# First x load in the set-up, flag sum, next layer norm and keep load inside the first stage's tail, weights loaded by the second stage

## The chip, the cores and the metric

One core of one Trainium2 chip runs the whole program. The metric is the device time of one execution in microseconds (us); about 14 us (0.5%) is what a measurement of this kernel can tell from no change. The engines are TensorE (PE, with its weight loads PEld), VectorE (DVE), ScalarE (ACT), GpSimd (POOL) and SyncE (SP, which issues every data transfer here).

## What is computed

Sixteen graphs (G = 16) of N = 1024 nodes with 128 features. Two layers, each with a residual:

```
h = max(layernorm(x), 0)
for W, b in three:                      # layer 0
    h = h @ W + b;  nh = h / max(|h|, 1e-12)
    h = (adj * (nh @ nh.T)) @ h         # relu after the first two
x = x + h                               # x1 below
h = max(layernorm(x), 0)                # layer 1
keep = dilate(adj > 0, mask)            # row by row, 1024 sequential steps
adj_d = adj * keep
h1, h2, h3 = three times: bn(relu(sage(., adj_d)))   # agg / degree, two projections, row norm
x = x + (concat(h1, h2, h3) @ Wl + bl) * mask
```

`keep` depends on `adj` alone. `bn` needs statistics over all graphs, so layer 1 is cut into stages.

## The kernel before, in words

The program is a row of blocks. In each block every engine runs its own list in order, and the block ends when all engines have come to its end: a barrier. The blocks are: `setup` (constants, the mask), `layer0`, `changed`, `dilate_all` under a condition, `weights`, `layer1_first`, `layer1_second`, `layer1_third`, `final`.

**layer0** does layer 0 of all graphs and, between its steps, the dilation. A graph is three units (`UNITS`, 48 in all, two graphs side by side). One step of a unit is `cos` (a 128x512 piece of nh nh^T: three matmuls on PE into one of two PSUM banks), then the product with adj on DVE into one of four `ew` buffers, then `agg` (PE). A `cos` on PE waits for the product two steps back, an `agg` for its own product. The kernel is written out from a plan: `Planner.order` takes steps with a cost, a rank and what they come after, and gives each engine its list. The names in it are: `lna` and `lnb` (layer norm on DVE: statistics, then subtract and scale), `lnc` (transpose of it), `posta` and `postb` (transpose of the result on PE, add to x on DVE; then SP stores x1), `fill` and `row` (the loads of adj for the dilation; a `fill` is then turned into 8 bits by POOL, a `row` by ACT), `base`, `rank`, `rule`, `drop`, `wide` (the dilation of a block of rows), `check` (writes a flag if a block's rounds did not settle), and `mask` (four transposes on PE, one DVE operation, and a store of 64 KB of keep from one of three `kp` buffers). Each SP list is strict: a load that waits holds back all behind it. The block ends on SP with waits for the last x1 store and the last keep stores.

**changed** is a block of its own: DVE sums the flags, PE adds them over the partitions with a matmul, DVE writes the integer `flag`. Then all engines load `flag` into a register and jump over `dilate_all` if it is 0, as it is here.

**weights** is a block with three loads by SP (W 768 KB, rows 640 KB as a broadcast, cols), on which its end waits; DVE fills `onesf` and `mf2`.

**layer1_first** takes the graphs in `ORDER` (14, 15, 0, 1, ...; the adj of graphs 14 and 15 is still in SBUF). For n = 0, `load(0)` brings x1 and keep of graph 14; DVE's `prep(0)` does its layer norm and then eight products adj * keep (`mk`, L1388); PE's first aggregation needs ReLU of the layer norm (`ln(0)` on ACT) and these products one by one; POOL adds the eight products for the degree (`dsum`), which PE sums at L1304; the projections with `W` come behind that.

Of the kernel before, what the change touches and what calls it, by code (L numbers as in the profile page):

```python
# [11 lines left out]
U8 = mybir.dt.uint8  # L12
# [90 lines left out]
def build(nc, A):  # L103
    with ExitStack() as top:
# [14 lines left out]
        C["flag"] = sb("flag", [128, 1], I32)  # L119
# [6 lines left out]

        C["adj"] = [sb(f"adj{i}", [128, NK, N]) for i in range(2)]
        setup(nc, A, C)
        layer0(nc, A, C, S)
        unsettled = changed(nc, C)  # L130
# [11 lines left out]
        weights(nc, A, C)  # L142
# [9 lines left out]
def setup(nc, A, C):  # L152
    with ExitStack() as ctx:
# [22 lines left out]
        def dve(e):  # L176
            e.memset(C["eps"][:], 1e-5)
            e.memset(C["flags"][:], 0.0)
# [20 lines left out]


def weights(nc, A, C):
    with ExitStack() as ctx:
        P = Scope(nc, ctx, "w")
        S = P.sems("loads")

        def sp(e):
            e.dma_start(C["W"][:], A["W"]).then_inc(S["loads"], 16)
            e.dma_start(C["rows"][:], A["rows"].partition_broadcast(128)).then_inc(S["loads"], 16)
            e.dma_start(C["cols"][:], A["cols"]).then_inc(S["loads"], 16)
            e.wait_ge(S["loads"], 48)  # L210

        def dve(e):
            e.memset(C["onesf"][:], 1.0)
            e.tensor_tensor(C["mf2"][:], C["mf"][:], C["mf"][:], ALU.mult)

        run(nc, dve=dve, sp=sp)
# [97 lines left out]
def plan_units(P):  # L314
# [10 lines left out]
    def prepare(v):  # L325
# [4 lines left out]
        if i == 0:  # L330
            if g > 1:
                transfer(("lnload", g), 1400, [("pe", "hf", v - 1)], rank=1)
            x = ("dma", "xfirst", 1) if g == 1 else ("dma", "lnload", g)
            add("dve", ("lna", g), 2070, 1, soon + [x])
# [26 lines left out]
    def agg(idx):  # L361
# [20 lines left out]
    post(3 * G - 2, [("pe", "agg", 16 * (3 * G - 1) + 1)])  # L382
    post(3 * G - 1, [])
# [69 lines left out]
def layer0_plan():  # L453
    P = Planner()
    plan_units(P)
    plan_dilation(P)
    return P.order({"D0": 1, "D1": 1, "ats0": 1, "ats1": 1, "af": 3, "v": 3, "kp": 3})


def layer0(nc, A, C, S):  # L460
    with ExitStack() as ctx:
# [3 lines left out]
        T = P.sems("ats0 ats1 at af0 af1 af2 sign low au x bs b0 ct ru vr sd v8 wb wd av rw tr kp kps0 kps1 kps2")  # L465
# [7 lines left out]
        tmp = P.sb("tmp", [128, NK, 128])  # L473
# [9 lines left out]
        ats = [P.sb(f"ats{i}", [128, 4, 128]) for i in range(2)]  # L483
        af = [P.sb(f"af{i}", [128, 512]) for i in range(3)]
# [47 lines left out]
        def sp(e):  # L532
# [3 lines left out]
            for kind, *a in plan["sp"]:  # L536
# [5 lines left out]
                elif kind == "lnload":  # L542
                    g, = a
                    if g:
                        e.wait_ge(E["tnh"], 6 * (g // 2) + g % 2)
# [3 lines left out]
                elif kind == "xload":  # L549
                    g, = a  # L550
                    if g == 0:
                        e.wait_ge(E["lnr"], 2)
                    else:
                        e.wait_ge(E["xs"], 16 * g)
                    e.dma_start(flat2(xt), A["x"][g]).then_inc(E["xld"], 16)
# [4 lines left out]
                elif kind == "fill":  # L560
# [4 lines left out]
                    e.dma_start(ats[h][:], A["adjT"][quad * Q + i][half(h), blk(k)].rearrange(  # L565
                        "(q p) n -> p q n", p=128)).then_inc(T[f"ats{h}"], 16)
                elif kind == "row":
# [4 lines left out]
                    e.dma_start(af[r % 3][:], A["adj"][n // NK * Q + i, blk(n % NK), half(j)]).then_inc(  # L572
                        T[f"af{r % 3}"], 16)
                elif kind == "mask":
# [4 lines left out]
                        T[f"kps{c % 3}"], 16)  # L579
            e.wait_ge(E["xs"], 16 * G)  # L580
# [3 lines left out]
        def pool(e):  # L584
            for kind, *a in plan["pool"]:
# [4 lines left out]
                e.tensor_scalar(TT[:, Q * (quad % 2) + i, 4 * h:4 * h + 4, blk(k)].bitcast(U8), ats[h][:], 0.0, ONE8,  # L590
                                ALU.is_gt, ALU.mult).then_inc(T["at"], 1)

        def pe(e):
# [11 lines left out]
            def take(bank, step):  # L605
                if users[bank]:
# [5 lines left out]
                    elif kind == "wide":  # L612
                        e.wait_ge(T["av"], nth["act", "wide", a[0], a[1], a[2]])
                    else:
                        e.wait_ge(T["kp"], nth["dve", "mask", a[0], a[1], a[2], a[3]])
# [1273 lines left out]
```

## Time and profile before

| what | value |
|---|---|
| median of 3 runs | 2811.43 us (2810.03 to 2820.57) |
| the profiled execution: its own time / its span | 2813.71 / 2811.9 us |
| PE / DVE / ACT / POOL busy | 2666.9 / 2183.0 / 1273.8 / 1092.8 us |
| mean granted TensorE clock | 0.981 |

The span runs from the first to the last instruction on the core; the execution's own time is 1.8 us longer. The profiled execution is 2.3 us above the median. Times in rows count from the start of the span.

### The profile page before, as it was taken

The numbers are of one execution on the slowest core, as the hardware profiler recorded it, in microseconds if no ns is written. First come the engines' busy times: TensorE is split into PE (matmuls) and PEld (weight loads), VectorE is DVE, ScalarE is ACT, GpSimd is POOL, SyncE is SP. The second block draws the span as 40 slices with busy tenths as digits, with TensorE's granted clock in tenths as the row PEclk, the third lists the DMA queues.
The fourth block names the chain that finished last, engine by engine and source line by source line (L and its number), as shares of the span: only waits on it lengthen the run. The fifth ranks groups of instructions, "written<-read, shape, count | busy, mean of one in ns | idle before, by whom it ended". The sixth has DMA issues, their size and how long they took to land. (4 is left out here: it accounts for less than half of the span.)

```text
span 2811.9 us, 41242 instructions
## 1 busy us (share of the span) xinstructions
PE 2666.9 (95%) x13446; PEld 1692.4 (60%) x13446; DVE 2183.0 (78%) x5582; ACT 1273.8 (45%) x3780; POOL 1092.8 (39%) x493
## 2 busy tenths in 40 slices
PE   6999999999999999999999968999999879999997
PEld 4666666666655656666666635555555545555886
DVE  5889999999888988999998857666666336774667
ACT  2555645665454454656544302333333324443664
POOL 3635344400143465730000008666666303442661
PEclk9999999999999999999999988999999989999998
DMA  6465374462273384562251133555555129996652
GB/s 231 150 213 188 105 218 148 126 218 70 84 255 105 114 287 134 167 220 82 63 187 53 34 99 116 200 200 201 201 201 202 65 96 397 394 396 239 223 201 121
DMA packets 322510, 492.31 MB, mean 175 GB/s; under 512 B 20592, under 2 KB 214512, under 8 KB 322288
## 3 DMA queue, kind: packets, MB, share of 16 engines
q1 hardware_dynamic: 322288, 489.57, 50.5%
q8 instruction: 112, 1.84, 0.3%
q14 instruction: 110, 0.90, 0.1%
HBM read 422.38 MB, written 67.11 MB: 174 GB/s over the span
## 5 line engine op out<-in xcount | busy, mean ns | idle before, releaser
L590 POOL TENSOR_SCALAR a_T<-a_ats 128x512 uint8<-128x512 f32 x256 | 514.8, 2019 | 711.7 <-DMA a_ats<-in_adjT 710.6
L668 PE MATMUL a_acc<-a_ew,a_Hr 128*128 128x512 f32 x1536 | 758.5, 602 | 0.0
L838 DVE TENSOR_TENSOR a_ew<-adj,a_cos 128x512 f32<-128x512 f32 x768 | 505.9, 679 | 37.8 <-PE a_cos L661 36.5
L659 PE MATMUL a_cos<-a_nh 128*128 128x512 f32 x768 | 407.4, 530 | 3.1 <-DVE a_nl L830 2.8
L1434 POOL TENSOR_TENSOR b_dsum<-adj 128x1024 f32<-128x1024 f32 x16 | 142.2, 8888 | 605.8 <-DVE adj L1388 605.8
L668 PEld LDWEIGHTS a_acc<-a_ew,a_Hr 128*128 128x128 f32 x1536 | 268.5, 190 | 140.5 <-issue 104.2
L767 ACT ACTIVATE a_vr<-a_D,a_small 128x128 f16<-128x128 f32 x560 | 210.1, 456 | 248.2 <-DVE a_small L902 247.9
L777 ACT ACTIVATE a_v<-a_D,a_wb,a_small 128x256 f16<-128x256 f32 x512 | 260.2, 561 | 119.0 <-PE a_D L702 108.1
L661 PE MATMUL a_cos<-a_nh,a_nl 128*128 128x512 f32 x768 | 304.1, 396 | 0.0
L660 PE MATMUL a_cos<-a_nl,a_nh 128*128 128x512 f32 x768 | 301.6, 393 | 0.0
L1278 PE MATMUL b_acc<-adj,b_h 128*128 128x512 f32 x512 | 224.3, 596 | 21.7 <-DVE adj L1388 21.7
L1438 POOL TENSOR_TENSOR b_dsum<-b_dsum,adj 128x1024 f32<-128x1024 f32 x96 | 225.7, 2351 | 14.4 <-POOL b_dsum L1438 0.9
L1278 PE MATMUL b_acc<-adj,b_z 128*128 128x512 f32 x512 | 224.1, 596 | 0.0
L1535 PE MATMUL c_acc<-adj,c_z 128*128 128x512 f32 x512 | 222.4, 592 | 0.0
L760 ACT ACTIVATE a_Ab<-a_af 128x512 fp8e4<-128x512 f32 x256 | 156.9, 632 | 92.2 <-DMA a_af<-in_adj 90.5
L1625 POOL TENSOR_TENSOR adj<-adj,c_kp 128x1024 f32<-128x1024 f32 x52 | 102.8, 2009 | 242.3 <-DMA adj<-in_adjT 242.3
L941 DVE SCALAR_TENSOR_TENSOR a_T<-a_v,a_Ab 128x512 fp8e4<-128x512 f16 x256 | 176.9, 706 | 24.3 <-ACT a_v L777 24.0
L659 PEld LDWEIGHTS a_cos<-a_nh 128*128 128x128 f32 x768 | 145.6, 190 | 66.0 <-issue 36.3
L951 DVE SCALAR_TENSOR_TENSOR a_kp<-a_D,a_T 128x512 fp8e4<-128x512 f32 x256 | 174.3, 684 | 11.7 <-PE a_D L715 8.9
L1278 PEld LDWEIGHTS b_acc<-adj,b_h 128*128 128x128 f32 x512 | 96.5, 191 | 138.0 <-issue 112.7
L660 PEld LDWEIGHTS a_cos<-a_nl,a_nh 128*128 128x128 f32 x768 | 146.5, 191 | 54.5 <-issue 43.8
L1278 PEld LDWEIGHTS b_acc<-adj,b_z 128*128 128x128 f32 x512 | 96.7, 191 | 115.9 <-issue 115.7
(205 smaller groups left out, 4467.5 us busy)
## 6 DMA issues: line engine op xcount, KB each, us to landing
adj<-in_adjT SPq DMA_DIRECT2D x108, 1024.0 KB, 12.6
adj<-in_adjT SPq DMA_DIRECT2D x128, 512.0 KB, 4.6
a_ats<-in_adjT SPq DMA_DIRECT2D x256, 256.0 KB, 3.3
a_af<-in_adj SPq DMA_DIRECT2D x256, 256.0 KB, 3.8
scr_keep<-a_kp SPq DMA_DIRECT2D x256, 64.0 KB, 1.5
b_kp<-scr_keep SPq DMA_DIRECT2D x16, 1024.0 KB, 7.3
c_zi<-scr_z SPq DMA_DIRECT2D x32, 512.0 KB, 6.0
c_ai<-scr_ag SPq DMA_DIRECT2D x32, 512.0 KB, 6.8
```

The costliest lines, as they stand in the source:

```text
L590: e.tensor_scalar(TT[:, Q * (quad % 2) + i, 4 * h:4 * h + 4, blk(k)].bitcast(U8), ats[h][:], 0.0, ONE8, ALU.is_gt, ALU.mult).then_inc(T["a ...
L659: e.matmul(cos[j][:], n[:, blk(k)], n[:, half(j)], start=True, stop=False)
L660: e.matmul(cos[j][:], n[:, blk(k)], m[:, half(j)], start=False, stop=False)
L661: e.matmul(cos[j][:], m[:, blk(k)], n[:, half(j)], start=False, stop=True).then_inc(E["cos"], 1)
L668: e.matmul(acc[j][:], Hr[u % 2][:, k, :], ew[idx % EW][:], start=(k == 0), stop=(k == NK - 1)).then_inc(E["agg"], 1)
L767: e.activation(vr[p][:, i, :], D0[:, i, :], ACT.Abs, bias=sm[p]["b2"][:, i:i + 1], scale=sm[p]["sc"][:, i:i + 1]).then_inc(T["vr"], 1)
L777: t = e.activation(v[c % 3][:, g * 256:g * 256 + 256], D1[:, 2 * g:2 * g + 2, :].rearrange("p b c -> p (b c)"), ACT.Abs, bias=wb[p][:, i, ...
L838: e.tensor_tensor(ew[idx % EW][:], adj[g % 2][:, k, half(j)], cos[j][:], ALU.mult).then_inc(E["ew"], 1)
L941: e.scalar_tensor_tensor(TT[:, slot, 4 * j:4 * j + 4, blk(k)], v[c % 3][:].rearrange("p (q c) -> p q c", c=128), 1.0, Ab[:, slot, half(j)] ...
L1278: t = e.matmul(acc[j][:], src[:, q, :], adj[n % 3][:, q, half(j)], start=(q == 0), stop=(q == NK - 1))
L1438: e.tensor_tensor(d[:], d[:], b[:, q, :], ALU.add).then_inc(E["ds"], 1)
L1535: t = e.matmul(acc[j][:], z[m % 2][:, q, :], adj[slot(m)][:, q, half(j)], start=(q == 0), stop=(q == NK - 1))
```

## The change

1. `setup`: SP's first transfer is now x of graph 0, ahead of the mask's. `lnload 0` leaves the plan; `lna 0` waits for `xload` instead. The buffer `tmp` is now `C["h0"]`, which lives through the program.
2. `changed` is gone. Its three steps are `tally` steps in layer0's plan, on the PSUM bank `D1` (a 1x1 matmul).
3. The layer norm of graph 14 for layer 1 is done in layer0, after `postb` of its own unit 46, from `xt` in SBUF: `lna 16`, `lnb 16` on DVE, square root and ReLU (`first`) on ACT. It is written to `C["h0"]`. The load of graph 15's x into `xt` (`xload 15`) now waits for `lnb 16`.
4. The keep load of graph 14 (1 MB) is issued by SP at the end of layer0, into `kp0`, which shares its space with the staging buffers of `fill` and `row`; it waits for the last keep store of graph 14. The end of the block doesn't wait for it.
5. `weights` is gone. Its loads are issued in layer1_first behind `load(1)`; PE and DVE wait for them (`wl`) at their first use. `prep(0)` is the eight products alone.
6. In the later stages some buffers have been laid on `C["h0"]`, `kp0` and `stage`.

```diff
@@ build
+        C["h0"] = sb("h0", [128, NK, 128])
+        C["stage"] = sb("stage", [128, 5, 512])
+        C["kp0"] = C["stage"][:, 0:4, :].rearrange("p a b -> p (a b)").bitcast(FP8).rearrange("p (k n) -> p k n", k=NK)
...
-        unsettled = changed(nc, C)
+        unsettled = nc.values_load(C["flag"][0:1, 0:1], min_val=0, max_val=128 * 128 * 128)
...
-        weights(nc, A, C)
@@ setup, sp
+            e.dma_start(flat2(C["h0"]), A["x"][0]).then_inc(C["xload"], 16)
             e.dma_start(mi[:], A["mask"]).then_inc(S["mask"], 16)
@@ plan_units
-            transfer(("xload", g), 1400, [("dma", "postb", UNITS.index((g - 1, 2)))] if g else [("dve", "lnb", 1)])
-
-    transfer(("lnload", 0), 1400, (), "sp")
+            read = [("dve", "lnb", G)] if g == G - 1 else []
+            transfer(("xload", g), 1400, read + ([("dma", "postb", UNITS.index((g - 1, 2)))] if g else [("dve", "lnb", 1)]))
...
     post(3 * G - 2, [("pe", "agg", 16 * (3 * G - 1) + 1)])
+    add("dve", ("lna", G), 2070, 1, [("dve", "postb", 3 * G - 2)])
+    add("act", ("lna", G), 210, 0, [("dve", "lna", G)])
+    add("dve", ("lnb", G), 2280, 1, [("act", "lna", G), ("pe", "hf", 3 * G - 1)])
+    add("act", ("first", 0), 920, 3, [("dve", "lnb", G)])
     post(3 * G - 1, [])
@@ layer0_plan
+    add("dve", ("tally", 0), 200, 3, [("dve", "check", n) for n in range(QUADS * NK)])
+    add("pe", ("tally", 1), 200, 2, [("dve", "tally", 0)], None, "D1")
+    add("dve", ("tally", 1), 200, 3, [("pe", "tally", 1)], None, None, "D1")
+    quad, i = divmod(ORDER[0], Q)
+    P.transfer(("keep", 0), 2800, [("dma", "mask", quad, i, q, j) for q in range(NK) for j in range(2)] +
+               [("act", "row", n, i, j) for n in range(NK * QUADS) for i in range(Q) for j in range(2)])
@@ layer0, sp
+                elif kind == "keep":
...
+                    for c in range(3):
+                        e.wait_ge(T[f"kps{c}"], max(16 * (m // 3 + 1) for m in stored if m % 3 == c))
+                    e.dma_start(C["kp0"].bitcast(U8), S["keep"][ORDER[0]].rearrange("k p n -> p k n")).then_inc(
+                        C["kpload"], 16)
@@ layer1_first, sp
-            load(0)
             load(1)
+            e.dma_start(C["W"][:], A["W"]).then_inc(E["wl"], 16)
+            e.dma_start(C["rows"][:], A["rows"].partition_broadcast(128)).then_inc(E["wl"], 16)
+            e.dma_start(C["cols"][:], A["cols"]).then_inc(E["wl"], 16)
             clear(e, C["bank"][0])
             load(2)
@@ layer1_first, dve
+            def prep(n):
+                b, c = adj[n % 3], kp[n % 2]
+                if n:
+                    norm(n)
+                if n:
+                    e.wait_ge(E[f"kp{n % 2}"], 16 * (n // 2 + n % 2))
+                else:
+                    e.wait_ge(C["kpload"], 16)
```

The two plans give the same lists except for swaps of neighbours among the first hundred steps and for the tail. DVE's list at the end of layer0, from `postb 46` on (the add to `a_x`), first of the kernel before; `a_ew` is the product of a step, `a_kp` a piece of keep:

```order
L843 TENSOR_TENSOR a_x<-a_pp,a_x 128x1024
L838 TENSOR_TENSOR a_ew<-adj,a_cos 128x512
L951 SCALAR_TENSOR_TENSOR a_kp<-a_D,a_T 128x512
L838 TENSOR_TENSOR a_ew<-adj,a_cos 128x512
L951 SCALAR_TENSOR_TENSOR a_kp<-a_D,a_T 128x512
L838 TENSOR_TENSOR a_ew<-adj,a_cos 128x512 x2
L951 SCALAR_TENSOR_TENSOR a_kp<-a_D,a_T 128x512 x2
```

The same place in the changed kernel (`h` is `C["h0"]`):

```order
L866 TENSOR_TENSOR a_x<-a_pp,a_x 128x1024
L861 TENSOR_TENSOR a_ew<-adj,a_cos 128x512
L816 BN_STATS a_lnst<-a_x 128x6 x8
L819 BN_AGGR a_lnmv<-a_lnst 128x2 x8
L861 TENSOR_TENSOR a_ew<-adj,a_cos 128x512 x2
L824 RECIPROCAL a_lnrs<-a_lnsd 128x8
L829 TENSOR_SCALAR h<-a_x,a_lnmv,a_lnrs 128x128 x8
L861 TENSOR_TENSOR a_ew<-adj,a_cos 128x512
L980 SCALAR_TENSOR_TENSOR a_kp<-a_D,a_T 128x512
L861 TENSOR_TENSOR a_ew<-adj,a_cos 128x512 x2
L980 SCALAR_TENSOR_TENSOR a_kp<-a_D,a_T 128x512 x2
```

The statistics stand between the products of steps 756 and 757, the subtraction between those of 758 and 759, and the mask pieces come later: the last of them is now behind the product of the last step, just ahead of the last `postb`.

SP's list at the end of layer0, before:

```order
L559 DMA scr_x<-a_x 128x1024
L578 DMA scr_keep<-a_kp 128x512 x2
L555 DMA a_x<-in_x 128x1024
L578 DMA scr_keep<-a_kp 128x512 x7
L559 DMA scr_x<-a_x 128x1024
L85 UNCONDITIONAL_BRANCH
```

and in the changed kernel (L588 is the keep load into `kp0`):

```order
L560 DMA scr_x<-a_x 128x1024
L556 DMA a_x<-in_x 128x1024
L579 DMA scr_keep<-a_kp 128x512 x10
L588 DMA stage<-scr_keep 128x8x1024
L560 DMA scr_x<-a_x 128x1024
L85 UNCONDITIONAL_BRANCH
```

The keep load stands directly ahead of the last x1 store, on whose landing the block's end waits, and the x load stands ahead of ten keep stores instead of seven.

## Rows read from the trace of the kernel before

**Rows 1.** Page, part 1: busy us (share of the span) xinstructions.
```profile
PE 2666.9 (95%) x13446; PEld 1692.4 (60%) x13446; DVE 2183.0 (78%) x5582; ACT 1273.8 (45%) x3780; POOL 1092.8 (39%) x493
```

**Rows 2.** Windows: us, busy of PE, PEld, DVE, ACT, POOL, PEclk, DMA share, GB/s.
```profile
4.00:35.00 31.00, 9.88 (x38) 8.31 (x39) 9.26 (x31) 6.20 (x21) 3.81 (x2) 0.85 0.97 356
...
1600.00:1660.00 60.00, 59.31 (x294) 36.07 (x292) 42.22 (x64) 6.13 (x23) 0.00 (x0) 1.00 0.17 50
1660.00:1688.00 28.00, 1.68 (x10) 1.35 (x10) 7.63 (x33) 1.36 (x2) 0.00 (x0) 0.57 0.52 175
```

**Rows 3.** Timeline of the start: start, us, engine, line, operation [idle before <-releaser].
```profile
0.75 0.39 SPq L160 DMA_DIRECT2D s_mi<-in_mask  x1
...
2.55 0.23 DVE L183 CAST mf<-s_mi 128x128 f32<-128x128 int32 x1 [0.88 <-DMA s_mi<-in_mask]
...
3.44 0.22 DVE L196 TENSOR_SCALAR UL<-s_t 128x128 bf16<-128x128 f32 x1
...
4.97 0.43 SPq L546 DMA_DIRECT2D a_tmp<-in_x  x1
...
10.82 1.65 DVE L793 BATCH_NORM_STATS2 a_lnst<-a_tmp 128x6 f32<-128x128 f32 x8 [7.17 <-DMA a_tmp<-in_x]
```

**Rows 4.** Timeline: the last fill that the first dilation block needs, and that block.
```profile
54.74 2.43 POOL L590 TENSOR_SCALAR a_T<-a_ats 128x512 uint8<-128x512 f32 x1 [0.26 <-DMA a_ats<-in_adjT]
...
57.23 0.86 PE L679 MATMUL a_D<-steps,a_T 128*128 128x6 bf16 x28
```

**Rows 5.** Timeline of layer0's tail.
```profile
1636.45 1.22 DVE L843 TENSOR_TENSOR a_x<-a_pp,a_x 128x1024 f32<-128x1024 f32 x1 [1.02 <-PE a_pp L596]
...
1655.03 0.39 PE L659 MATMUL a_cos<-a_nh 128*128 128x512 f32 x1
...
1655.72 3.59 PE L668 MATMUL a_acc<-a_ew,a_Hr 128*128 128x512 f32 x8
...
1661.13 1.22 DVE L843 TENSOR_TENSOR a_x<-a_pp,a_x 128x1024 f32<-128x1024 f32 x1 [4.53 <-PE a_pp L596]
1662.38 0.33 SPq L559 DMA_DIRECT2D scr_x<-a_x  x1
```

**Rows 6.** Page, part 5: all products of a step; busy, mean ns, idle before.
```profile
L838 DVE TENSOR_TENSOR a_ew<-adj,a_cos 128x512 f32<-128x512 f32 x768 | 505.9, 679 | 37.8 <-PE a_cos L661 36.5
```

**Rows 7.** Timeline between layer0 and the first aggregation of layer 1.
```profile
1665.50 0.17 DVE L970 MEMSET n_ones<- 128x128 f32 x1 [3.15 <-PEq L85]
...
1665.77 0.59 PE L967 MATMUL n_ps<-n_r,n_ones 128*128 128x1 f32 x2 [4.67 <-DVE n_r L971]
1666.39 0.16 DVE L973 CAST flag<-n_ps 128x1 int32<-128x1 f32 x1 [0.68 <-PE n_ps L967]
1670.88 0.35 SPq L207 DMA_DIRECT2D W<-in_W  x1
...
1678.63 0.33 SPq L1241 DMA_DIRECT2D b_x<-scr_x  x1
...
1681.86 1.65 DVE L1373 BATCH_NORM_STATS2 b_lnst<-b_x 128x6 f32<-128x128 f32 x8 [10.61 <-DMA b_x<-scr_x]
...
1684.42 0.20 DVE L1378 RECIPROCAL b_lnrs<-b_lnsd 128x8 f32<-128x8 f32 x1 [0.37 <-ACT b_lnsd L1321]
...
1686.71 9.16 DVE L1388 TENSOR_TENSOR adj<-adj,b_kp 128x1024 f32<-128x1024 f32 x8
...
1688.07 15.85 PE L1278 MATMUL b_acc<-adj,b_h 128*128 128x512 f32 x32 [21.72 <-DVE adj L1388]
```

**Rows 8.** Timeline: PE's sum of the degree of the first graph.
```profile
1713.17 3.57 PE L1304 MATMUL b_dp<-onesf,b_dsum 128*128 128x1 f32 x16 [8.37 <-POOL b_dsum L1438]
```

**Rows 9.** Windows, columns as in Rows 2: the keep loads of layer1_first's start.
```profile
1684.00:1688.00 4.00, 0.00 (x0) 0.00 (x0) 3.60 (x12) 1.36 (x2) 0.00 (x0) 0.50 1.06 380
```

**Rows 10.** DMA issues of the whole span: xcount, KB each, median us to landing.
```profile
scr_keep<-a_kp SPq DMA_DIRECT2D x256, 64.0 KB, 1.5
...
scr_z<-c_zT SPq DMA_DIRECT2D x16, 512.0 KB, 15.6
```

More of the change, by code:

```diff
@@ L198, in setup @@
         run(nc, dve=dve, pool=pool, sp=sp)
[L201 to L216, printed above, removed]
 def col8(t, g):
@@ L716, in pe @@
                     t.then_inc(T["tr"], 1)
+                elif kind == "tally":
+                    e.wait_ge(T["sum"], 1)
+                    take("D1", step)
+                    e.matmul(D1[0:1, 0, 0:1], tot[:], C["ones1"][:], start=True, stop=True).then_inc(T["tot"], 1)
         def act(e):
@@ L723, in act @@
                     e.activation(lnsd[:], lnmv[:, :, 1], ACT.Sqrt, bias=C["eps"][:, 0:1]).then_inc(E["lnsd"], 1)
+                elif kind == "first":
+                    e.wait_ge(E["lnr"], G + 1)
+                    e.activation(flat2(tmp), flat2(tmp), ACT.Relu).then_inc(E["relu"], 1)
                 elif kind == "lnc":
@@ L868, in dve @@
                                            saturate=False).then_inc(T["x"], 1)
+                elif kind == "tally" and a[0] == 0:
+                    e.wait_ge(T["v8"], QUADS * NK)
+                    e.tensor_reduce(tot[:], C["flags"][:], AXX, ALU.add).then_inc(T["sum"], 1)
+                elif kind == "tally":
+                    e.wait_ge(T["tot"], 1)
+                    e.tensor_copy(C["flag"][:], D1[0:1, 0, 0:1]).then_inc(T["flag"], 1)
                 elif kind == "base":
@@ L956, in layer0 @@
         run(nc, pe, act, dve, pool, sp)
-def changed(nc, C):
-    with ExitStack() as ctx:
-        P = Scope(nc, ctx, "n")
-        S = P.sems("sums total")
-        r, ones, ps = P.sb("r", [128, 1]), P.sb("ones", [128, 128]), P.ps("ps", [128, 1])
-        def pe(e):
-            e.wait_ge(S["sums"], 1)
-            e.matmul(ps[:], ones[:], r[:], start=True, stop=True).then_inc(S["total"], 1)
-        def dve(e):
-            e.memset(ones[:], 1.0)
-            e.tensor_reduce(r[:], C["flags"][:], AXX, ALU.add).then_inc(S["sums"], 1)
-            e.wait_ge(S["total"], 1)
-            e.tensor_copy(C["flag"][:], ps[:])
-        run(nc, pe=pe, dve=dve)
-    return nc.values_load(C["flag"][0:1, 0:1], min_val=0, max_val=128 * 128 * 128)
 def dilate_all(nc, A, C, S):
@@ L1163, in dilate_all, with sp @@
                 mask(q)
+        def sp(e):
+            e.dma_start(C["kp0"].bitcast(U8), S["keep"][ORDER[0]].rearrange("k p n -> p k n")).then_inc(E["load"], 16)
+            e.wait_ge(E["load"], 16)
+        stage(sp=sp)
 def adj_rows(A, g):
@@ L1208, in layer1_first @@
         P = Scope(nc, ctx, "b", C["bank"][1])
-        E = P.sems("x0 x1 kp0 kp1 " + " ".join(f"adj{s}{c}" for s in range(3) for c in range(4))
+        E = P.sems("x0 x1 kp0 kp1 wl one " + " ".join(f"adj{s}{c}" for s in range(3) for c in range(4))
                    + " bst bag lnsd lnrs lnr hr mk ds ag ev th hT tz zt bs zst0 zst1 a1st dgp dgm dgr dgc"
@@ L1388, in prep @@
                     e.tensor_tensor(b[:, q, :], b[:, q, :], c[:, q, :], ALU.mult).then_inc(E["mk"], 1)
+            e.memset(C["onesf"][:], 1.0).then_inc(E["one"], 1)
             prep(0)
+            e.tensor_tensor(C["mf2"][:], C["mf"][:], C["mf"][:], ALU.mult)
             for n in range(G + 1):
@@ L1448, in layer1_second @@
         adj = C["adj"]
-        kp = [P.sb(f"kp{i}", [128, NK, N], FP8) for i in range(3)]
+        kp = [C["kp0"]] + [P.sb(f"kp{i}", [128, NK, N], FP8)[:] for i in (1, 2)]
         o = [P.sb(f"o{i}", [128, NK, 128]) for i in range(2)]
@@ L1453, in layer1_second @@
         zi = [P.sb(f"zi{i}", [128, N]) for i in range(3)]
-        ai = [P.sb(f"ai{i}", [128, N]) for i in range(3)]
+        ai = [flat2(C["h0"])] + [P.sb(f"ai{i}", [128, N])[:] for i in (1, 2)]
         a2 = [P.sb(f"a2{i}", [128, N]) for i in range(2)]
```

120 lines of the change are left out of this document (72 added, 48 removed).

## The prediction

> **What bounds the kernel now.** I read the busy shares first, then the windows, then the timeline at the three places that the change touches. PE is busy for 95% of the span [rows 1]: there is little to gain but where PE stands still. In layer0's last 60 us PE is busy for 59.31, and DVE for 42.22, so that stretch is PE's [rows 2]. Two holes stand out. At the start PE works 9.88 of 31 us while the DMA engines are 97% busy [rows 2]; the layer norm that everything waits for starts at 10.82, after 7.17 us of waiting for x, whose transfer was only issued at 4.97 [rows 3]. And between 1660 and 1688 PE works 1.68 of 28 us [rows 2]. The timeline of that hole is a chain without a fork [rows 7]: layer0 ends (DVE goes on at 1665.50), flags summed to 1666.55, a jump to 1670.88, the weights to 1678.63, x1 to 1681.86, the layer norm, and the first product at 1686.71, with PE 1.36 us behind it. The change works on both holes, and pays for it in the tail between them.
>
> **The hole after layer0.** From the end of layer0 to the first product it is 1686.71 - 1665.50 = 21.21 us now [rows 7]. In the changed kernel the register load and the jump stay: 1670.88 - 1666.55 = 4.33 us [rows 7]. Then DVE fills `onesf` (0.17 us; the same size as the fill at 1665.50 [rows 7]) and starts the products, as nothing else is left ahead of them: 4.5 us. Flag block (1.05), weights (7.75), x1 load (3.23) and layer norm with its waits (4.85) are gone: 21.2 - 4.5 = **16.7 us gained**. What follows hangs on the products as before: PE began 1.36 us after the first of them, which is one product, so its wait for the ReLU had hidden nothing. The weights are issued behind x1 and keep of graph 15 (1.6 MB), 3.0 MB in all, or 7.9 us at the 380 GB/s of [rows 9]; today the three loads alone take 7.75 us from the first issue to the block's end. PE wants them only behind its degree sum, 1713.17 - 1686.71 = 26.5 us after the first product [rows 7, 8]. They cost nothing; if that cover were gone they would cost the 7.75 us again. x1 of graph 15 is wanted after the eight products (9.16 us) and takes 3.2: covered. The price of the jump is the one thing here that I take over whole. It holds nothing that depends on the block behind it by any row, so I take 4.33, with 0 to 4.3 more.
>
> The Trainium skill speaks against that: "Runtime: NRT & Kernel Launch", section "Instruction fetch mechanics", says that a taken branch to code outside the fetched pages stops the engine until a fetch has brought them. By that rule the 7.75 us of the weights block may have covered fetches of the next block's code, which would now show. No row quoted here says what the 4.33 us consist of; I keep it as a rival.
>
> **The start.** x is now issued at about 0.75, and the mask 0.4 us behind it. x alone took 3.23 us in the quiet queue at 1678.63 [rows 7], so it lands near 4.0, and the mask, which took 1.80 us when alone [rows 3], right behind x at about 4.2. Set-up's DVE work behind the mask, 2.55 to 3.66 [rows 3], moves by 1.65 us, and so does the block's end. The statistics can start near 3.95 + 1.65 = 5.6 instead of 10.82: **5.2 us gained**. x is there by then: the mask is late next. If x took the 5.85 us that it took behind other loads [rows 3], it would be 4.2. Does the gain reach the end? The unit's own chain (PE, ACT, DVE by turns) moves with it. The dilation's loads don't: the queue is full until about 35 us [rows 2], it starts 1.65 us later and has x's 0.5 MB (1.5 us at 356 GB/s) less, so its end stays. The first dilation block on PE came at 57.23, just behind the eighth fill, which ended at 57.17 [rows 4]. It must move to 52.1. After 35 us the queue has room, and these fills wait for each other and for SP, which was held by the second x load until `lnb 1` (moving with the chain); I count them on to about 52 us too. Bounds: 3.6 to 6 us.
>
> **The tail of layer0.** It gets 4.5 us of DVE work: statistics 1684.42 - 0.37 - 1681.86 = 2.19 us, subtraction 1686.71 - 1684.42 = 2.29 us [rows 7]. DVE has 18 of 60 us free there [rows 2], 7 us in the 23 us from `postb 46` to the last agg, so the sum fits; but each half holds back a product. PE takes 0.69 us for a cos (1655.03 to 1655.72) and 0.90 for an agg (3.59 / 4) [rows 5]. Count from 1636.45, where the transposes let DVE go on [rows 5]: PE has cos 756 and 757 done at 1637.8, agg 754 and 755 at 1639.6, cos 758 at 1640.3, then cos 759 waits for product 757. DVE: add to 1637.7, product 756 (0.68 [rows 6]) 1638.35, statistics 1640.55, product 757 1641.2. PE stands 0.9 us. By the same count it stands 0.5 us at cos 761, which waits for product 759 behind the subtraction. Together **1.4 us lost**; 0 if PE's slack is a little larger, 4.5 if none of it hides. The mask pieces that move behind have the last agg and ACT's copies as cover (PE's last transposes end at 1661.13, 1.8 us after the last agg at 1659.31 [rows 5]). `tally` adds its matmul to PE, 0.59 us [rows 7], in a full stretch: **0.6 us lost**; its two DVE steps (0.3 us) fit in DVE's room. SP stands at `xload 15` until `lnb 16` has ended; behind it are keep stores, and DVE's third piece on waits for them, but DVE comes to these pieces only after `lnb 16`: nothing.
>
> The keep load (1.05 MB, 2.8 us at 380 GB/s [rows 9]) goes on the queue just ahead of the last x1 store, for whose landing the block waits: now 1662.38 to 1665.50, 3.1 us [rows 5, 7]. The last keep piece comes behind the last agg (1659.31), DVE 0.7 us, SP 0.33 us; the store it must wait for lands in 1.5 us [rows 10] and was issued before. So the load is issued about 1.5 us ahead of the x1 store, and the store waits for what is left: 2.8 - 1.5 = **1.3 us lost**, from 0 (if both share the engines without delay) to 2.8. DVE will not wait for it after the jump: it was issued some 9 us before the first product.
>
> **Sum.** -16.7 - 5.2 + 1.4 + 0.6 + 1.3 = -18.6 us. Against the profiled execution's own time, 2813.71, that is 2795.1; that execution stands 2.3 us above the median of the three runs, so beside the median 2811.43 I expect **2793 us**. Layer 1 from its second graph on, and the later stages, only have other addresses: 0.
>
> **The rivals.**
> - *The jump costs more* (the page's rule above as a mechanism of this kernel: engines fetch the code of layer1_first while nothing waits now, and will do so on the path). Price up to another 4.3 us, the length of the whole jump today [rows 7]: 2797. For it: the weights block is 7.75 us in which PE and ACT do nothing. Against: the block's own code starts right behind the jump today too. Chance 0.12.
> - *The start's gain is lost in the dilation* because the fills stay where the full queue puts them: PE waits for them at its first dilation block until 57.2 [rows 4]. Price 5.1 us, total -13.5: 2798. For it: the 0.06 us between fill and block, so they are already equal. Against: these fills come 20 us after the queue has emptied. Chance 0.12.
> - *The layer norm isn't hidden* in the tail, and the x1 store waits for all of the keep load: 4.5 instead of 1.4 and 2.8 instead of 1.3, total -14: 2797.5. Chance 0.08.
> - *Slower than before*: the last x1 store, stuck behind the keep load at the end of the block. It decides from a landing of 3.1 + 1.3 + 18.6 = 23 us on; the slowest kind of transfer in the trace lands in 15.6 us, where the queue is full [rows 10], and here it is 17% busy [rows 2]. Chance 0.02.
> - *It doesn't do what it says*, that is, another chain of the same length stands beside the one removed: none of the engines has other work in the hole [rows 2]. Chance 0.02.
>
> **How the numbers follow.** My forecast has 0.64. Its own range comes from the bounds: the start 3.6 to 6, the tail's three terms 1 to 5 with one of them off, the jump within 1 us: 2788 to 2797. The rivals end between 2797 and 2798, and one of them with another term off at 2802, so the range is 2788 to 2801. About 14 us (0.5%) is what a measurement can tell from no change; that is 2797.4. The forecast lies below it but for a tenth, and half of the first and third rival: 0.76 faster, 0.21 within, 0.03 slower.
>
> **What would show it.** Right: the first statistics of `C["h0"]` at 5 to 6.5 us; the first dilation block on PE near 52 us; two DVE groups of 2.2 us behind `postb 46` with PE idle under 1 us at each; the last x1 store landing 3 to 6 us after issue; between the first action after layer0 and the first product under 5 us. Wrong: a jump of 6 us or more, a wait of PE or POOL for a fill at 50 to 60 us, a first product that waits for the keep load, PE waiting for `wl`, or PE at its lower clock (1.2 GHz) for longer than now when the first aggregation starts.

## The result, and the profile after

| | before | after |
|---|---|---|
| median (16 runs each) | 2811.98 us (2808.85 to 2820.57) | 2800.04 us (2794.69 to 2808.02) |
| profiled execution: its own time / span | 2813.71 / 2811.9 us | 2807.94 / 2805.9 us |

The ratio of the times is 0.9958, with a 95% interval of [0.9951, 0.9966]: 11.9 us (0.4%) are gained. Forecast were 18.6 us, a time of 2793.0 and a range of 2788 to 2801. The time is inside the range and the direction is right, but a third of the gain is missing. By the line that the prediction drew at 2797.4 (0.5%), the result is not yet "faster" but "within", to which it gave 0.21; only the 16 runs on each side, with an interval below 1, show the gain. The profiled execution of after is 8 us above its median; section by section it can be read, but its span as a whole understates the gain.

I read the changed kernel at the same places. The start, where [rows 3] waited for x until 10.82 (timeline; start, us, engine, line, operation, idle before and its releaser):

```profile
0.75 0.39 SPq L164 DMA_DIRECT2D h<-in_x  x1
...
1.20 0.41 SPq L165 DMA_DIRECT2D s_mi<-in_mask  x1
...
4.51 0.23 DVE L189 CAST mf<-s_mi 128x128 f32<-128x128 int32 x1 [2.80 <-DMA s_mi<-in_mask]
...
5.91 1.64 DVE L816 BATCH_NORM_STATS2 a_lnst<-h 128x6 f32<-128x128 f32 x8 [0.30 <-PEq L85]
```

The statistics start 4.91 us earlier (forecast 5.2), and what they waited for last is the end of set-up behind the mask, not x. (The 3.95 us at which the prediction lets set-up end stands in none of its rows; the trace has ACT's first instruction behind it at 3.92.) Then the first dilation block, which stood at 57.23 in [rows 4]:

```profile
56.65 0.86 PE L691 MATMUL a_D<-steps,a_T 128*128 128x6 bf16 x28 [1.01 <-POOL a_T L600]
```

It has moved by 0.58 us, not by 5.1, and PE waits 1.01 us for the last fill. This was on my list of what would show the forecast wrong; the experiments show below how much of it is this one trace. The tail, against [rows 5]:

```profile
1638.37 1.23 DVE L866 TENSOR_TENSOR a_x<-a_pp,a_x 128x1024 f32<-128x1024 f32 x1 [1.03 <-PE a_pp L606]
...
1640.10 1.64 DVE L816 BATCH_NORM_STATS2 a_lnst<-a_x 128x6 f32<-128x128 f32 x8
...
1642.91 0.50 PE L671 MATMUL a_cos<-a_nh 128*128 128x512 f32 x1 [0.51 <-DVE a_ew L861]
...
1643.60 2.15 DVE L829 TENSOR_SCALAR h<-a_x,a_lnmv,a_lnrs 128x128 f32<-128x128 f32 x8
...
1664.19 1.23 DVE L866 TENSOR_TENSOR a_x<-a_pp,a_x 128x1024 f32<-128x1024 f32 x1 [0.80 <-PE a_pp L606]
1665.45 0.33 SPq L560 DMA_DIRECT2D scr_x<-a_x  x1
```

From one `postb` to the other it is 1664.19 - 1638.37 = 25.82 us, against 24.68 in [rows 5]: the layer norm costs 1.14 us (forecast 1.4). PE shows one marked wait of 0.51 us. The hole, against [rows 7]:

```profile
1676.79 0.17 DVE L1421 MEMSET onesf<- 128x128 f32 x1 [11.37 <-issue]
1676.87 19.84 DVE L1419 TENSOR_TENSOR adj<-adj,stage 128x1024 f32<-128x1024 f32 x8
...
1679.24 3.25 POOL L1469 TENSOR_TENSOR b_dsum<-adj 128x1024 f32<-128x1024 f32 x1 [450.24 <-DVE adj L1419]
1682.64 18.76 POOL L1473 TENSOR_TENSOR b_dsum<-b_dsum,adj 128x1024 f32<-128x1024 f32 x6
```

The chain of flag sum, weights, x1 and layer norm is gone: from the last x1 store's issue to the first product it is 1676.87 - 1665.45 = 11.42 us, against 1686.71 - 1662.38 = 24.33 in [rows 5, 7]. But the eight products take 19.84 us instead of the 9.16 of [rows 7], and PE waits for them. The same execution, PE:

```profile
1686.91 1.84 PE L1297 MATMUL b_acc<-adj,h 128*128 128x512 f32 x2 [2.10 <-DVE adj L1419]
...
1696.76 10.00 PE L1297 MATMUL b_acc<-adj,h 128*128 128x512 f32 x18 [1.21 <-DVE adj L1419]
...
1707.47 1.84 PE L1326 MATMUL b_dp<-onesf,b_dsum 128*128 128x1 f32 x16
```

From the fifth product on, each pair of aggregations waits 1.2 to 2.1 us for its product; the graph's aggregation ends 29.9 us behind the first product (1706.76), against 17.2 us before (1703.92 in [rows 7]). Before, PE then had 8.37 us to wait for the degree ([rows 8], 26.5 us behind the first product); now it goes on without a wait. So of 12.7 us that the aggregation is late, 9.3 had been idle anyway, and about 3.4 remain. The count is rough, as what follows isn't alike either: behind its wait PE's degree sum took 3.57 us before [rows 8] and takes 1.84 now, and by the reciprocal of the fourth graph's degree this trace is 3.0 us behind (B below). PE's granted clock shows the same stretch (windows of after; us, busy of PE, PEld, DVE, ACT, POOL, PEclk, DMA share, GB/s):

```profile
1683.00:1688.00 5.00, 2.84 (x5) 0.65 (x4) 5.00 (x3) 0.00 (x0) 4.85 (x2) 0.84 1.03 397
1688.00:1693.00 5.00, 2.83 (x3) 0.50 (x2) 5.00 (x2) 0.00 (x0) 4.71 (x3) 0.50 0.14 54
1693.00:1698.00 5.00, 3.31 (x4) 1.22 (x5) 5.00 (x3) 0.00 (x0) 4.86 (x2) 0.50 0.05 2
```

In the kernel before the clock was at 1.00 (2.4 GHz) from 1692 to 1704, from 4 us behind the first aggregation's start to its end. Here it rises for a moment, PE stands still in between, and it is back at 0.50 (1.2 GHz) until 1698. Nothing in the prediction's sum had this; its list named the longer stretch at the lower clock as a sign of something wrong. The landings of the transfers between 1655 and 1685 us (count, KB each, median us from issue to landing):

```profile
stage<-scr_keep SPq DMA_DIRECT2D x1, 1024.0 KB, 6.4
...
scr_x<-a_x SPq DMA_DIRECT2D x1, 512.0 KB, 6.1
```

The same store in the kernel before:

```profile
scr_x<-a_x SPq DMA_DIRECT2D x1, 512.0 KB, 2.6
```

The store on which the block's end waits lands 3.5 us later after its issue (forecast 1.3). So of the 11.42 us, 6.1 are the store and 5.3 the jump; of the 24.33, 2.6 were the store and 21.7 the chain behind it.

### The profile page after: what moved, and what is told of

It reads as the page before. It is cut to its first block and busy times, and to the rows that moved or that the text cites. A ratio compares the mean times of both kernels' runs of the same rounds, so it can differ in the third digit from the quotient of the medians.

```text
span 2805.9 us, 41224 instructions
## 1 busy us (share of the span) xinstructions
PE 2676.0 (95%) x13446; PEld 1690.8 (60%) x13446; DVE 2195.6 (78%) x5582; ACT 1274.3 (45%) x3780; POOL 1090.1 (39%) x493
## 5 line engine op out<-in xcount | busy, mean ns | idle before, releaser
L600 POOL TENSOR_SCALAR a_T<-stage 128x512 uint8<-128x512 f32 x256 | 513.4, 2013 | 713.3 <-DMA stage<-in_adjT 711.0
L1469 POOL TENSOR_TENSOR b_dsum<-adj 128x1024 f32<-128x1024 f32 x16 | 136.5, 8534 | 600.4 <-DVE adj L1419 600.4
L779 ACT ACTIVATE a_Ab<-stage 128x512 fp8e4<-128x512 f32 x256 | 157.0, 632 | 93.5 <-DMA stage<-in_adj 92.0
L1570 PEld LDWEIGHTS c_acc<-adj,c_z 128*128 128x128 f32 x512 | 96.1, 190 | 114.8 <-issue 112.6
L673 PEld LDWEIGHTS a_cos<-a_nh,a_nl 128*128 128x128 f32 x768 | 144.5, 188 | 33.2
L754 ACT ACTIVATE h<-a_Hr 128x128 f32<-128x128 f32 x384 | 113.5, 300 | 68.0 <-DVE a_Hr L839 67.8
## 6 DMA issues: line engine op xcount, KB each, us to landing
adj<-in_adjT SPq DMA_DIRECT2D x108, 1024.0 KB, 12.7
```

The costliest lines, as they stand in the source:

```text
L673: e.matmul(cos[j][:], m[:, blk(k)], n[:, half(j)], start=False, stop=True).then_inc(E["cos"], 1)
L1570: t = e.matmul(acc[j][:], z[m % 2][:, q, :], adj[slot(m)][:, q, half(j)], start=(q == 0), stop=(q == NK - 1))
```

## The experiments

The kernel before ran beside each group: medians of 2811.58, 2813.39, 2809.77 (one run) and 2811.89 us. Two quantities are read in each trace. A: from the issue of the last x1 store to the first product. B: from the first product to the reciprocal of the fourth graph's degree, which shows what the beginning of layer 1 costs PE. In the kernel before A is 24.33 and B is 136.53 us; after, 11.42 and 139.48.

**The changed kernel again, unchanged.**

> The changed kernel once more, for a second trace. Theory A (the start's gain is lost in the dilation): the first dilation block on PE again at 56 to 57 us, behind the eighth fill, and unit 3 of layer0 again within 1 us of the kernel before. Theory B (the profiled execution lost it by chance): unit 3 is 3 to 5 us ahead of the kernel before. In both, the eight products of the first graph of layer 1 take 19.8 us again, if what slows them is a property of the program and not of one execution.

2801.25 us, ratio 0.9954 [0.9939, 0.9968]; A 10.93, B 140.23, eight products in 19.84 us. The store's landing (6.0 us) and the slow products repeat. The start doesn't: the first dilation block comes at 55.59, and unit 3 is 3.8 us ahead of the kernel before (the start of its last operation, `a_nl`: 110.41 for 114.19), as theory B has it, while in the first trace it was 0.2 us ahead. Layer0 as a whole doesn't repeat either: its last `postb` starts at 1659.26 here and at 1664.19 above, with the same lists. Over all traces it lies between 1650.6 and 1664.2. Terms of 1 to 3 us inside layer0 can't be read from where layer0 ends in one trace; they are read from their place, or from medians.

**The start alone**, on the kernel before.

```diff
@@ build, setup: C["h0"] as in the change
+            e.dma_start(flat2(C["h0"]), A["x"][0]).then_inc(C["xload"], 16)
             e.dma_start(mi[:], A["mask"]).then_inc(S["mask"], 16)
@@ plan_units: lna 0 waits for nothing of the plan
-    transfer(("lnload", 0), 1400, (), "sp")
```

> The kernel before with nothing but the first x load moved into the set-up. Theory A (gain lost in the dilation): the first layer norm starts near 5.9 us instead of 10.8, but unit 3 within 1 us, and the time within 1.5 us of the kernel before. Theory B (gain kept): 4 to 5 us faster than the kernel before.

2808.68 us, ratio 0.9988 [0.9977, 1.0]: 2.9 us by the medians, 3.4 by the ratio. The last operation of unit 0 (`a_nl`) starts 4.4 us earlier than before (26.85 for 31.28), that of unit 1 only 2.8 us earlier (56.94 for 59.73), and unit 3's 2.4 us. Neither theory holds: the gain lies between the two, with an interval from 0 to 6.5 us. The products are undisturbed (9.17 us), A is 24.16.

**The changed kernel without the start.**

```diff
@@ setup, sp
-            e.dma_start(flat2(C["h0"]), A["x"][0]).then_inc(C["xload"], 16)
@@ layer0, sp, behind W and rows
+            e.dma_start(flat2(C["h0"]), A["x"][0]).then_inc(C["xload"], 16)
```

> The changed kernel, with the first x load back in layer0's own list, as in the kernel before (behind W and rows; the set-up loads only the mask). If the start's gain is the 2.9 us that the start alone brought, this kernel is about 3 us slower than the changed one, near 2803 us, and its first statistics begin near 10.8 us; if the 5.2 us of the first statistics reached the end whole, it is 5 us slower, near 2805 us. If the start brings nothing, it is as fast as the changed one (2800 us).

2803.52 us, ratio 0.9966 [0.9952, 0.9979]. Statistics start at 11.05. Against 0.9958 and 0.9954 the start is worth 0.0008 to 0.0012, or 2.2 to 3.4 us, near the 2.9 of the other side; but the intervals overlap, so the times alone can't tell 2.9 from 4.9. The traces say more. The last operation of unit 0 starts at 26.5 to 26.9 us in the eleven traces with x moved and SP's list unchanged, against 31.3 and 31.8 in the two without (the kernel before and this one): 4.8 us by the means. That of unit 1 starts at 55.5 to 58.4 (mean 56.9) against 59.7 and 60.5: 3.3 us. That of unit 2 comes at 77.7 to 82.5 (mean 79.5) against 82.0 and 82.7: 2.9 us. The first dilation block stands at 59.72 here, and at 54.7 to 58.0 (mean 56.2) in the eleven: set against both traces without the move it comes 2.3 us earlier, so the 0.58 us above is one pair of traces.

**Store ahead of the keep load.**

```diff
@@ layer0, sp: the step "keep" does nothing; its waits and its load stand behind the loop over the plan
+            e.dma_start(C["kp0"].bitcast(U8), S["keep"][ORDER[0]].rearrange("k p n -> p k n")).then_inc(
+                C["kpload"], 16)
```

> The changed kernel with the last x1 store ahead of the keep load on SP's list. Theory: the store behind the keep load costs 2.4 us (it landed about 5.5 us after its issue instead of 3.1), so this is 2.4 us faster than the changed kernel, with the first product at most 9 us after the store's issue. Rival: the jump after it is bound by the queue (code is fetched while the keep load still moves), so the first product doesn't come earlier: 0 to 0.5 us faster.

2796.96 us, ratio 0.9938 [0.9922, 0.9953]. The landings in its trace:

```profile
stage<-scr_keep SPq DMA_DIRECT2D x1, 1024.0 KB, 6.7
...
scr_x<-a_x SPq DMA_DIRECT2D x1, 512.0 KB, 3.1
```

A is 8.61. The store lands 3.0 us sooner than with the keep load ahead. The time is 3.1 us below the changed kernel's, with intervals that just touch. A falls by 2.2 us only (the mean of the eight traces with the changed order is 11.0, of the four with this one 8.8, to the first operation of DVE where others stand ahead of the products): the stretch behind the landing grows from 5.0 (4.6 to 5.3) to 5.7 us (5.4 to 6.0), while the keep load still moves. The products still take 19.84 us.

**POOL's first sum behind all eight products** of the first graph.

```diff
-                e.wait_ge(E["mk"], 8 * n + 2)
+                e.wait_ge(E["mk"], 8 * n + (2 if n else 8))
```

> The changed kernel, but POOL starts the degree sum of the first graph only when all eight products are done. Theory: DVE and POOL take turns at the SBUF and each product takes 3.3 us; then here the products take 9.2 us, the sum 7 times 2.35 us behind them (done 26 us after the first product, against 24.5), and the steady state is reached 2 to 3 us earlier than in the changed kernel. Rival: the turns cost nothing, since the sum of the degree sets the pace of the first graph: within 1 us of the changed kernel, or 1.5 us slower.

2797.71 us, ratio 0.9946 [0.9931, 0.9961]. The eight products take 9.11 us again and B is 136.29. So the 19.84 us come from POOL's sums, and the difference in B is their price on the path (the time alone, 2.3 us below the changed kernel, is within the intervals): 3.2 us here, and 3.5 between the means of the seven traces with the full turns (139.9) and of the six without any (136.4).

**Both edits.**

> The changed kernel with both single edits of the runs before: the last x1 store ahead of the keep load, and POOL's first sum of the first graph behind all eight products. My theory says that the two costs (2.3 us of the store's wait, 3.7 us of products that take turns with POOL) lie one behind the other on the path: so 2800.5 - 6 = 2794 us, with 8.6 us from the last x1 store to the first product and eight products of 9.2 us in all. Rival: both edits remove the same wait, since each alone gave about 3.5 to 4 us; then it stays at 2797.

2790.61 us, ratio 0.9923 [0.9909, 0.9937]: 22.8 us below the kernel before, and the lowest median of all. The interval reaches from 2786 to 2794 us: it shuts out the rival's 2797 and holds the 2794 expected, though only at its edge. So the two costs add up. A is 9.09 us in this trace (8.6 expected). Its hole and first products:

```profile
1652.65 0.33 SPq L560 DMA_DIRECT2D scr_x<-a_x  x1
1653.16 0.39 SPq L591 DMA_DIRECT2D stage<-scr_keep  x1
1661.47 0.32 SPq L1260 DMA_DIRECT2D b_x<-scr_x  x1
...
1661.74 9.10 DVE L1422 TENSOR_TENSOR adj<-adj,stage 128x1024 f32<-128x1024 f32 x8
...
1662.95 16.23 PE L1300 MATMUL b_acc<-adj,h 128*128 128x512 f32 x32 [11.59 <-DVE adj L1422]
```

**Fills ahead of rows**, on the kernel with both edits: SP's list at the start.

```diff
@@ layer0_plan; before: xload, row, fill, row, fill, row, row, row, fill, fill
+    new = [("fill", 0, 0, 2, 0), ("fill", 0, 0, 2, 1), ("xload", 0), ("row", 0, 1, 1), ("fill", 0, 0, 3, 0),
+           ("row", 0, 2, 0), ("fill", 0, 0, 3, 1), ("row", 0, 2, 1), ("row", 0, 3, 0), ("row", 0, 3, 1)]
+    sp[at:at + 10] = new
```

> The kernel with both edits, and on SP's list at the start the four last fills that the first dilation block needs stand ahead of rows, and two of them ahead of the second x load. If the start's gain is lost because PE waits at that block for fills that keep their time, the block moves from near 56 us to near 52 and the end moves with it: 2 us less than the kernel with both edits, near 2792. If the gain is lost elsewhere in layer0, the block moves and the end doesn't; if the rows, now later, are waited for in their place (ACT holds them ahead of its own steps), it becomes slower by 1 to 3 us.

2793.17 us, ratio 0.9927 [0.9913, 0.9941], the same within the intervals. The fills are done earlier (the eighth by 51.45 instead of 54.77), but the dilation block comes at 57.24, later than the 54.92 of the kernel with both edits, and PE doesn't wait for a fill any more. What is late now are the rows, for which ACT waits:

```profile
45.44 0.63 ACT L789 ACTIVATE a_Ab<-stage 128x512 fp8e4<-128x512 f32 x1 [2.33 <-DMA stage<-in_adj]
48.29 0.63 ACT L789 ACTIVATE a_Ab<-stage 128x512 fp8e4<-128x512 f32 x1 [2.22 <-DMA stage<-in_adj]
```

With both edits alone the same two waits are 1.44 and 1.11 us. Through them unit 1's own chain is late (58.04 for 55.72). So the fills are not the only limit; no kernel was run with the rows earlier, and that they take the rest of the start's gain is read from traces alone. In the changed kernel (ACT):

```profile
40.67 1.02 ACT L748 ACTIVATE a_hT<-a_pp 128x1024 f32<-128x1024 f32 x1 [1.55 <-PE a_pp L606]
...
46.80 0.63 ACT L779 ACTIVATE a_Ab<-stage 128x512 fp8e4<-128x512 f32 x1 [2.48 <-DMA stage<-in_adj]
47.34 0.29 ACT L754 ACTIVATE h<-a_Hr 128x128 f32<-128x128 f32 x1
```

and in the kernel before:

```profile
45.21 1.02 ACT L729 ACTIVATE a_hT<-a_pp 128x1024 f32<-128x1024 f32 x1 [3.78 <-PE a_pp L596]
...
49.59 0.63 ACT L760 ACTIVATE a_Ab<-a_af 128x512 fp8e4<-128x512 f32 x1 [0.99 <-DMA a_af<-in_adj]
50.12 0.29 ACT L735 ACTIVATE a_tmp<-a_Hr 128x128 f32<-128x128 f32 x1
```

`a_hT` of unit 1 comes 4.54 us earlier, the squares (L754) only 2.78 us: ahead of them on ACT's list stand two `row` steps, which wait 1.48 and 2.48 us for their transfers here, and 1.21 and 0.99 us before. In this trace the 4.54 us become 2.78 at these two instructions.

**What makes the products slow.** Five kernels with more work on DVE ahead of the products, or with another start for POOL; all but the third are the changed kernel with the edit alone, and none changes what is computed.

Sixteen fills of 128x128 ahead:

```diff
+            for k in range(16):
+                e.memset(o[k // NK][:, k % NK, :], 0.0)
             prep(0)
```

> The changed kernel, with sixteen fills of 128x128 with zeros on DVE (into buffers that are written again before they are read) ahead of the first of the eight products of the first graph. They take some 2 us on the path. Theory A: the products and POOL's sums take turns because DVE has run nothing long since the jump and POOL starts while DVE's products come in the first few us behind it; with 2 us of other work ahead, the turns vanish and the eight products take 9.2 us instead of 19.8. Theory B: it is what stands directly ahead of the products (a fill instead of the layer norm's subtraction) that decides; then the turns stay here.

Eight products in 19.84 us, B 139.58; 2808.55 us (one run). It isn't the time since the jump.

Eight operations of the layer norm's form ahead:

```diff
+            for k in range(NK):
+                e.tensor_scalar(o[0][:, k, :], C["h0"][:, k, :], C["mf"][:, 0:1], C["mf"][:, 1:2], ALU.subtract, ALU.mult)
             prep(0)
```

> The changed kernel, with eight operations of the layer norm's form (subtract and multiply, 128x128, from the layer norm's result into a buffer that is written again before it is read) on DVE ahead of the eight products of the first graph; 2.3 us on the path. Theory B (what stands directly ahead of the products decides): the turns with POOL vanish, eight products in 9.2 us. Theory A (the time since the jump): they vanish here and behind sixteen fills too. If they stay in both, neither is it.

```profile
1667.07 2.03 DVE L1423 TENSOR_SCALAR b_o<-h,mf 128x128 f32<-128x128 f32 x8
...
1669.02 9.17 DVE L1419 TENSOR_TENSOR adj<-adj,stage 128x1024 f32<-128x1024 f32 x8
```

```profile
1671.46 9.14 POOL L1471 TENSOR_TENSOR b_dsum<-adj 128x1024 f32<-128x1024 f32 x1 [450.35 <-DVE adj L1419]
1680.75 2.34 POOL L1475 TENSOR_TENSOR b_dsum<-b_dsum,adj 128x1024 f32<-128x1024 f32 x1
```

The turns are gone: products in 9.17 us, B 136.46, 2797.39 us (one run), and POOL's first sum is stretched over the products, as in the kernel before, where it took 8.94 us.

One such operation ahead (`for k in range(1)`), with the store ahead of the keep load:

> The changed kernel with the last x1 store ahead of the keep load, and ONE operation of the layer norm's form (subtract and multiply, 128x128, into a buffer that is written again before it is read) on DVE between the fill of onesf and the eight products of the first graph. If one such operation directly ahead is enough for the products to run back to back, the eight take 9.2 us, POOL's first sum is stretched to about 9 us, and the kernel is as fast as the one with both edits (0.992 of the kernel before, near 2791 to 2794 us). If it takes several, the eight products take 19.8 us, as after sixteen fills, and the kernel stays at 0.994, near 2797.

Products in 19.90 us, B 139.68; 2799.17 us, ratio 0.9951 [0.9938, 0.9965]. One isn't enough.

Eight such operations, then the fill of `onesf`, then the products:

```diff
-            e.memset(C["onesf"][:], 1.0).then_inc(E["one"], 1)
             for k in range(NK):
...
+            e.memset(C["onesf"][:], 1.0).then_inc(E["one"], 1)
             prep(0)
```

> The changed kernel with the same eight operations of the layer norm's form on DVE, but with the fill of onesf between them and the products. If what stands directly ahead of the first product decides, the turns come back (eight products in 19.8 us). If it is enough that such operations ran some time since the jump, they stay away (9.2 us).

Products in 19.84 us, B 139.27; 2809.68 us (one run). One fill between them and the products brings the turns back.

**POOL's first sum behind the fourth product** (`2 if n else 4`).

> The changed kernel, with POOL's first sum of the first graph behind the fourth product instead of the second. If the turns come because POOL steps in at a moment when DVE is between its first, short-queued products, they vanish: POOL's first sum is then stretched until the eighth product has ended, as in the kernel before. If they come whenever POOL has a sum while DVE multiplies in this stretch, products five to eight take 3.4 us each, and all eight some 15 us instead of 19.8.

```profile
1662.88 15.54 DVE L1419 TENSOR_TENSOR adj<-adj,stage 128x1024 f32<-128x1024 f32 x8
...
1667.52 3.25 POOL L1469 TENSOR_TENSOR b_dsum<-adj 128x1024 f32<-128x1024 f32 x1 [450.62 <-DVE adj L1419]
```

15.54 us, with products six to eight at 3.36 us each. The turns come whenever POOL has a sum while DVE multiplies in this stretch; they begin at the sixth product and not at the fifth, as POOL's first sum is there only when the fifth has started. (By its own "products five to eight" the expectation would have come to some 18 us, not 15.) PE waits 0.35, 2.15 and 2.15 us for products, and its aggregation ends 26.1 us behind the first product, still just within the 26.5 us at which the kernel before had its degree: B is 135.73. In this trace the turns cost nothing, as they only use up that reserve. 2789.09 us (one run, with the shortest layer0 of all traces).

## Why the prediction was right in direction and 7 us off in size

| term | forecast us | measured us | from |
|---|---|---|---|
| hole, with the jump | -16.7 | -16.7 | 21.7 behind the landing before, 5.0 after (mean of eight traces) |
| x1 store behind keep load | +1.3 | +3.4 | landing 2.6 before, 6.0 after |
| layer norm in the tail | +1.4 | +1.14 | 24.68 and 25.82 |
| tally | +0.6 | not measured | not run alone; 0.6 is taken over into the sum |
| start | -5.2 | -2.9 | the start alone; 2.2 to 3.4 from the other side; unit 2 in the traces 2.9 |
| products in turns with POOL | not foreseen | +3.5 | B with and without; 3.4 by the count above |
| sum | -18.6 | -11.0 | -11.9 by the medians |

That the time lies in the range is in part luck. The forecast's own range ended at 2797; the 2800 is covered only because the rivals stretched the range to 2801, and of the 7 us that are missing 3.5 belong to a term that no rival named, while the sum's own misses, 2.3 us at the start and 2.1 at the store, go the same way. The chances don't add up as written either: 0.64 less a tenth of it, and half of 0.12 and of 0.08, make 0.68 faster and some 0.3 within, not 0.76 and 0.21. And by the prediction's own words one of its cases ends at 2802, outside its 2801.

**The hole** came as worked out. The jump kept its price: 5.0 us behind the landing in the changed kernel (4.6 to 5.3 in eight traces). Counted from the same landing, the forecast had 4.5 + 0.5 = 5.0, and the kernel before has 4.33 [rows 7] + 0.52 us (from the landing at 1664.98 to 1665.50), with the flag block between. "Runtime: NRT & Kernel Launch", section "Instruction fetch mechanics", of the Trainium skill says that a taken branch whose target is not in the fetched window waits for a fetch. The traces agree that something is fetched, and show that it is not new. The packets of the DMA queues have a kind called `instruction` (queue, kind: packets, MB, share of 16 engines). In the kernel before, from 1666.6 to 1670.8:

```profile
q14 instruction: 4, 0.03, 2.9%
q8 instruction: 1, 0.02, 2.7%
```

and in the changed kernel, from 1671.6 to 1676.5:

```profile
q14 instruction: 4, 0.03, 2.2%
q8 instruction: 1, 0.02, 1.2%
```

The same five packets fall into the jump before (1668.22 to 1670.30) and after (1673.40 to 1675.11), so the weights block behind the jump had not covered them. The next such packets come as the next block begins, in both (from 1670.82 and from 1676.53), and no wait of the first products for them shows. So the first rival is false. Where the keep load still moves, the first of these packets comes 2.2 to 2.4 us behind the landing instead of 1.8 to 1.9: most of the extra 0.7 us passes before any of them. Why is open.

**The store behind the keep load** was mis-sized: "the store waits for what is left: 2.8 - 1.5". That counted the keep load as moving from its issue on. The windows say otherwise (after; us, busy of PE, PEld, DVE, ACT, POOL, PEclk, DMA share, GB/s):

```profile
1664.00:1666.00 2.00, 0.16 (x2) 0.00 (x0) 1.23 (x1) 0.00 (x0) 0.00 (x0) 1.00 0.44 88
1666.00:1668.00 2.00, 0.00 (x0) 0.00 (x0) 0.00 (x0) 0.00 (x0) 0.00 (x0) 0.68 0.91 254
1668.00:1670.00 2.00, 0.00 (x0) 0.00 (x0) 0.00 (x0) 0.00 (x0) 0.00 (x0) 0.50 1.03 379
1670.00:1672.00 2.00, 0.00 (x0) 0.00 (x0) 0.00 (x0) 0.00 (x0) 0.00 (x0) 0.50 0.24 98
```

The load is issued at 1663.94 and the store at 1665.45, but by 1666 only 88 GB/s x 2 us = 0.18 MB have moved, and 0.065 MB of that is a keep store. Nearly all of the 1 MB moves beside the store's 0.5, at 254 GB/s first and not at 380. So the store pays for the whole load, at its lower rate: 3.4 us, above the 2.8 that I had as the upper bound (that half of the third rival came true). It was one step of SP's list. Exchanging it brings the landing back to 3.1 us, and 2.2 us of that reach the first product.

**The layer norm** is hidden as counted, and alike in all twelve traces that have it (25.82 to 25.86 us). The other half of the third rival is false.

**The start** failed at "I count them on to about 52 us too". The second rival was half right: the block at 57.23 moved by 0.58 us in this trace, and lies between 0.8 us later and 2.5 us earlier in the others with that list (by the means of the traces it moved by 2.3 us, and the time by 2.9, so the gain isn't lost whole). But its mechanism was incomplete. With the fills earlier the time stayed, and the traces show why: the rows, which share SP's list and the queue, are waited for by ACT ahead of unit 1's own steps. I had followed only the loads that PE waits for, not those that stand in ACT's list.

**What was not in the sum**: that the eight products take as long as before. I took "What follows hangs on the products as before" from [rows 7] without asking what stood ahead of them. POOL adds up the products while DVE makes them. In the kernel before, DVE kept going and POOL waited; with the layer norm moved away, a product and a sum take turns, 3.3 us for the pair, from the fourth product on. The removed work was not only a cost: standing directly ahead of the products, it went with the pattern in which POOL waits (the experiments show that such operations there are enough, not why). POOL's sums are wanted 26.5 us after the first product [rows 7, 8], DVE's products at once; the kernel before had it the right way round by accident.

Weights, `wl`, `kpload` and x1 of graph 15 cost nothing, as forecast: no wait for them shows in the trace. The rival that the time becomes longer is false.

## What to carry to other kernels

When a block that only delays is taken out, ask of each engine which instruction will now stand directly ahead of the first of the next block, and who works beside it: the durations of the rows belong to that neighbourhood. Put the transfer on whose landing a barrier waits ahead of the bulk transfer that nobody needs yet, even if the bulk transfer is then issued later; a load issued 1.5 us ahead is not 1.5 us ahead in bytes. And a gain at the start of a long chain is cut at every list that the chain passes and in which something else, a load of another task above all, has not moved with it.

## What the runs showed of the hardware

DVE and POOL on the same data get in each other's way in one of two patterns, and which one it is isn't given by the two instructions. DVE multiplies 128x1024 f32 (1.22 us alone) and POOL adds 128x1024 f32 (2.35 us alone):

- *held*: DVE's products run back to back, eight in 9.16 us, and POOL's first sum is stretched to 8.94 to 9.14 us, until they have ended (before, the start alone, eight operations ahead).
- *turns*: each product takes 3.36 us and each sum 3.13 to 3.25 us, by turns, a pair every 3.28 us; even a product of 128x128 behind them takes 2.43 instead of 0.29 us (after, and seven further traces).

POOL arrives at the same point of the third product in both, 2.37 to 2.44 us behind the first one's start. "SBUF — State Buffer", section "Who interferes with whom", of the Trainium skill says that a VectorE instruction with two SBUF inputs and a GpSimd instruction that reads SBUF exclude each other for the whole instruction, and that issue order decides. The traces agree for one instruction, though not to the full (a product takes 1.22 us, and 3.36 when a sum stands between; the pair's 3.28 us is 0.3 less than 1.22 + 2.35, so a little of the two overlaps). Which engine comes next when both have work waiting comes out either way here. Eight subtract-and-multiply operations directly ahead give the held pattern in all three kernels that have them for the first graph. The products of the other fifteen graphs stand behind a layer norm in every kernel, and in all 14 traces they are held (eight in 9.15 to 9.17 us, first sum 8.87 to 8.96). For the first graph one such operation, sixteen fills, or eight with one fill behind give turns. Why is open: the runs show the condition, not the cause, and nothing between one such operation and eight was run.
